# GpSimd's normalisation moved to step 6, and the PE's two score products of a step exchanged, in a two-layer transformer stack on one core

## The reference

```python
def _L0_attn_b_ref(x, Wqkv, Wo):
    qkv = (x @ Wqkv).reshape(b, l, 3, H, DH)          # H = 16 heads of DH = 16
    q, k, v = (qkv[:, :, 0], qkv[:, :, 1], qkv[:, :, 2])
    q = q * cos + rotate_half(q) * sin
    k = k * cos + rotate_half(k) * sin
    scores = jnp.einsum('bqhd,bkhd->bhqk', q, k) * scale
    attn = jax.nn.softmax(scores, axis=-1)
    out = jnp.einsum('bhqk,bkhd->bqhd', attn, v)
    return out.reshape(b, l, d) @ Wo
```

## Time and profile before

| what | value |
|---|---|
| runs | 2940.69, 2942.93, 2943.54 us (median 2942.93) |
| the profiled execution | 2938.81 us, of which the span is 2937.1 us |
| PE busy over the span | 2314.2 us (79%) |
| DVE, ACT, POOL busy | 1943.5 (66%), 1537.0 (52%), 912.0 us (31%) |
| granted PE clock, mean | 0.902 of full speed |
| stage rope | 967 to 1435 us |
| stage latent | 2152 to 2649 us |

### The profile page before, as it was taken

One profiled execution on the slowest core, in us unless ns is written; L12 is line 12 of the kernel. 1 busy time (PEld: TensorE's weight loads), 2 busy tenths in 40 slices (PEclk: granted clock), 3 DMA queues, 4 the chain that ended last, 5 costly groups with the idle time before them and its releaser, 6 DMA issues. The chain is left out here.

```text
span 2937.1 us, 40653 instructions
## 1 busy us (share of the span) xinstructions
PE 2314.2 (79%) x13550; PEld 1158.7 (39%) x13550; DVE 1943.5 (66%) x4549; ACT 1537.0 (52%) x2426; POOL 912.0 (31%) x851
## 2 busy tenths in 40 slices
PE   5899999998575899998756786399578788884698
PEld 2344444443452233332345555266322222223365
DVE  5788888886536888888463344577487677774343
ACT  2477766676523576777642333355146566672122
POOL 0333222230232344443033201355144445413111
PEclk7799999999887899999888898699779999996799
DMA  7665656550254112112126002454411211203232
GB/s 243 187 188 174 185 175 181 174 168 23 92 184 125 45 50 61 46 54 56 49 84 193 24 1 87 164 215 179 152 39 52 53 45 50 60 24 143 92 135 83
DMA packets 193506, 318.32 MB, mean 108 GB/s; under 512 B 29285, under 2 KB 155272, under 8 KB 188564
## 3 DMA queue, kind: packets, MB, share of 16 engines
q1 hardware_dynamic: 177764, 266.31, 29.1%
q0 software_dynamic: 15536, 49.41, 4.9%
HBM read 164.41 MB, written 151.59 MB: 108 GB/s over the span
## 5 line engine op out<-in xcount | busy, mean ns | idle before, releaser
L1816 DVE CUSTOM_DVE_ANT_0 decay_junk<-decay_scores_q,decay_corr 128x512 bf16<-128x512 f32 x512 | 338.3, 684 | 112.8 <-PE decay_scores_q L1553 110.6
L1733 ACT ACTIVATE decay_probs<-decay_scores_k 128x512 f32<-128x512 f32 x512 | 294.7, 597 | 190.4 <-PE decay_scores_k L1572 154.3
L2503 DVE TENSOR_REDUCE latent_mx<-latent_scores 128x2 f32<-128x1024 f32 x256 | 310.1, 1222 | 111.0 <-PE latent_scores L2292 110.7
L2426 ACT ACTIVATE latent_probs<-latent_scores,latent_escale 128x1024 f32<-128x1024 f32 x256 | 282.3, 1116 | 189.8 <-PE latent_scores L2305 189.0
L2426 ACT ACTIVATE rope_probs<-rope_scores,rope_escale 128x1024 f32<-128x1024 f32 x256 | 283.5, 1116 | 152.4 <-PE rope_scores L2305 151.6
L2503 DVE TENSOR_REDUCE rope_mx<-rope_scores 128x2 f32<-128x1024 f32 x256 | 311.1, 1223 | 78.7 <-PE rope_scores L2292 77.6
L1553 PE MATMUL decay_scores_q<-decay_KS,decay_QS 96*128 96x512 bf16 x512 | 204.8, 401 | 37.1 <-DVE decay_mx L1816 22.9
L1569 PE MATMUL decay_scores_k<-decay_QS,decay_KS 99*128 99x384 bf16 (+3 forms) x512 | 157.0, 308 | 14.4 <-DMA decay_QS<-decay_mT 6.6
L1597 PE MATMUL decay_out_heads<-decay_probs,decay_Vaug 128*32 128x512 f32 x1024 | 143.3, 633 | 0.8 <-DVE decay_probs L1828 0.8
L2318 PE MATMUL latent_out_heads<-latent_probs,latent_Vaug 128*32 128x512 f32 x1024 | 137.2, 608 | 6.7 <-ACT latent_Osb L2417 4.1
L2318 PE MATMUL rope_out_heads<-rope_probs,rope_Vaug 128*32 128x512 f32 x1024 | 137.2, 608 | 6.0 <-ACT rope_Osb L2417 4.1
(11 more groups left out here) (455 smaller groups left out, 5137.4 us busy)
## 6 DMA issues: line engine op xcount, KB each, us to landing
decay_KS<-decay_parts_dram SPq DMA_DIRECT2D x64, 384.0 KB
decay_QS<-decay_parts_dram SPq DMA_DIRECT2D x64, 384.0 KB
decay_parts_dram<-decay_parts SPq DMA_DIRECT2D x56, 384.0 KB, 3.1
experts3x_w<-in_w_dram SPq DMA_DIRECT2D x16, 1024.0 KB, 11.1
weight_parts<-experts3x_w SPq DMA_DIRECT2D x8, 2048.0 KB, 7.5
experts4x_w<-weight_parts SPq DMA_DIRECT2D x8, 2048.0 KB, 8.1
decay_parts_dram<-decay_parts SPq DMA_DIRECT2D x56, 256.0 KB, 3.3
experts_xin<-dispatched SPq DMA_DIRECT2D x96, 128.0 KB
```

The costliest lines, as they stand in the source:

```text
L1733: act.activation(probs[:, (b * 16 + kk) % PSLOTS, h, :], psB[:, s % 2, :], ACT.Exp, scale=scale).then_inc(exp_done, 1)
L1816: dve.tensor_tensor_reduce(junk[:, a % 2, :], psA[:, A_BANK[k], :], corr[:, qt, :], 1.0, -3.0e38, ALU.mult, ALU.max, mx[:, grp % 2, qt, h: ...
L2426: act.activation(probs[:, kk % 2, 2 * (u % 2):2 * (u % 2) + 2, :], psS[:, slot_of("exp", n), :, :], ACT.Exp, scale=escale[:, 0:1]).then_in ...
L2503: dve.tensor_reduce(mx[:, grp % 2, :, hp, qt], psS[:, slot_of("top", n), :, :], AX.X, ALU.max).then_inc(a_done, 1)
```

## The change

Two things. In both layers GpSimd normalises at step 6 and not at 18: behind its second rotary chain and not behind its third. And in each step the PE issues the score product for the maxima ahead of the one for the exponentials, with the list that gives out the PSUM slots changed alike. In `scores`, `top` is a tile for maxima and `exp` one for the exponential.

```diff
     ROTATE_AT = [2, 4, 16, 18]
-    NORMALISE_AT, PV_AT = 18, 1
+    NORMALISE_AT, PV_AT = 6, 1
...
     scores = [("top", n) for n in range(16)]
     for n in range(NB * STEPS):
-        scores += [("exp", n)] + ([("top", n + 16)] if n + 16 < NB * STEPS else [])
+        scores += ([("top", n + 16)] if n + 16 < NB * STEPS else []) + [("exp", n)]
     place = {x: i for i, x in enumerate(scores)}
...
             for b in range(NB):
                 for u in range(STEPS):
-                    exp_scores(b, u)
                     if top_of(b, u) is not None:
                         max_scores(top_of(b, u))
+                    exp_scores(b, u)
                     if u % 2 == PV_AT:
```

## The result

The changed kernel takes **2910.7 us** (median of six runs, 2906.7 to 2925.1); the kernel before took 2939.2 beside it (2935.6 to 2943.5). The ratio is 0.991, with the interval 0.9887 to 0.9932. Forecast were 2900 us within 2876 to 2924, faster. The profiled execution has a span of 2913.2 us, against 2937.1.

A forecast was written before the change was run, and what follows sets the result against it. The PE, fullest engine in rope and latent, was held by its standstills, chiefly a DMA wait in latent. -52 in latent, -5.8 in rope and +15 for the order gave -43 us: 2942.9 to 2900 us, range 2876 to 2924.

The forecast's parts named there:

- The long wait: Latent's batch boundaries: six PE waits for the row maxima's DMA, 37.4 us, caused by GpSimd normalising before its fourth chain.
- The clock term: Latent, PE work behind each long wait: the lower clock costs 2.66 us, six times, 16.0 us to be won back.
- The ports' rival: DVE's MV copies and row splits wait for GpSimd in crowded steps: +14 to +28 us, 2914 to 2928; chance 0.15.
- The order: Max scores ahead of exp scores in each step: costs 1.3 to 1.4 us a rope batch, 0.75 a latent batch, +15 us.
- the walk by start-to-start spacings: All 32 steps of a middle rope batch: new stalls not ACT's 4.7 us against 5.4; 1.56 lost behind the output additions.
- the sentence on latent: Latent has no q products: scalings cost nothing, steps 2 and 16 wait 0.4 more for a copy, +0.75 us a batch.
- below 1.2 us each: Both layers: the PE's other waits, for DVE or ACT to empty a PSUM bank or slot, are short, below 1.2 us.
- part 1: Normalise moved to step 6 in GpSimd's idle time: -52 us in latent (45 to 55) and -5.8 in rope.
- What would show it: Confirming signs: DMA wait gone, exp scores' waits for maxima 30 us or more per layer, latent near 450, rope within 6 of 468.
- signs that I was wrong: A DVE copy at L2545 over 0.17, third chain later than step 16's shuffle, or rope shorter by over 8 us.
- The order is cheap or a gain: Rival: the exchanged score order costs zero (2885 us) or wins 1 us a batch (2869); chance 0.20.
- Slower: Rival: exp scores make the PE pay all DVE work, +96 us, 2981; decides from 3.6 us a batch; chance 0.04.

The follow-up runs named there:

- norm_only: The changed kernel with normalise still at step 6 but the old order of the score products: 2882.5 us.
- norm_tripled: norm_only, with GpSimd in latent writing sixteen more normalised halves into an unread spare tile ahead of the real ones: 2919.9 us.
- order_only: The changed kernel with the new order of score products but normalise back at step 18: 2939.4 us, ratio 1.0005 to the kernel before.
- rotate_later: The changed kernel with the DVE's third and fourth rotation at steps 17 and 19 instead of 16 and 18: 2905.0 us.
- change_again: The changed kernel run once more without an edit, for its spread and a second profile: 2905.1 us.
- statistics_later: The changed kernel with the statistics of the two output additions put off to steps 15 and 17 of the next batch: 2898.1 us.
- heads_first: norm_only, with the DVE emptying the turned heads ahead of the step's maxima: 2860.1 us.
- sums_first: heads_first, with the addition to X also ahead of the maxima and its statistics behind them: 2843.6 us, ratio 0.9671 to the kernel before.

## Why the prediction was right, and where it wasn't

**The long wait: right.** The boundary's chain (GpSimd's normalisation ahead of the fourth chain, the parts' writes ahead of the rows' in SP's queue) was the cause; norm_only removes the wait whole and norm_tripled, by filling the same idle time, brings it back. Latent -47.2 lies within my 45 to 55, rope -7.2 beside the 5.8. The clock term holds in kind: the two steps behind a 6.6 us wait took 2.66 us more, the product behind 3.8 us 1.5 more. In size it was too large: of the 47.2, 37.4 are the waits themselves, which leaves 9.8 and not 16.0 for the clock and all else. I allowed only 1.4 for what is won back behind a wait; that the rest is such gain is inferred from the difference.

**The ports' rival: there, but too small to count.** The copies to MV (L2545), of the whole run and both layers: minimum, median and maximum in ns.

```profile
L2545 DVE COPY X<-rope_mv x16: 170/170/171, 1047.7 to 1454.7; 128x4 f32<-128x4 f32 x16
L2545 DVE COPY X<-latent_mv x16: 170/171/505, 2243.5 to 2638.6; 128x4 f32<-128x4 f32 x16
```

The medians hide some longer ones. Fifteen of the 32 copies began while a TENSOR_SCALAR of GpSimd ran. Nine of them kept their 0.17, and six, all in latent, took 0.28 to 0.51, five of these until 0.02 to 0.03 us behind the end of GpSimd's instruction. Here are the two of one batch; the normalisation, shown above, ends at 2359.05 + 6.51 = 2365.56:

```profile
2361.08 0.17 DVE L2545 COPY X<-latent_mv 128x4 f32<-128x4 f32 x1
2365.31 0.29 DVE L2545 COPY X<-latent_mv 128x4 f32<-128x4 f32 x1
```

So the neighbours that I priced at nothing cost 1.0 us of DVE time in all, within the upper bound that I had named and far from the rival's 14 to 28. Beside a TENSOR_TENSOR of GpSimd the effect is larger: the split of order_only took 2.22 us beside the 2.36 of the bias. The Trainium skill (SBUF — State Buffer, "Who interferes with whom") says that, when a DVE instruction in a two-port mode and one of GpSimd meet, whichever of the two issues first has the shared pair for its whole instruction while the other is fully blocked; the 2.22 beside 2.36 agrees and so do five of the longer copies, the 0.17 beside GpSimd's TENSOR_SCALAR does not.

**The order: right in sign, wrong in size.** In a middle batch of rope it costs 60.39 - 59.16 = 1.23, forecast 1.3 to 1.4; so the walk by start-to-start spacings was good to 0.1. In latent it costs 58.74 - 57.18 = 1.56, forecast 0.75. The step that failed is the sentence on latent, in which I carried rope's walk over, took the cost of the scalings off and added 0.4 at each idle step. From the first exp scores of a step to those of the next, in a middle batch, the change is longer than norm_only by (us):

```
           steps 0-15   16-19   20-31   batch
rope          0.47       0.39    0.38    1.24
latent        0.46       0.71    0.39    1.56
```

So latent saves nothing on the scalings that it doesn't have: up to step 15 and from step 20 on it pays what rope pays. The rest is at steps 16 to 19, where the split and the shuffle hold up the maxima and the exp scores of step 18 wait 0.60 us; rotate_later takes 0.50 of it back.

A second term wasn't in the sum of the order at all, the clock. The walk found the 1.56 us wait at step 13 and counted it once. Here it is as measured in rope's second batch (PE), and busy time with the granted clock (the last three numbers are clock, DMA share and GB/s) just behind it and in rope's end:

```profile
1053.31 0.39 PE L2305 MATMUL rope_scores<-rope_QS,rope_KS 50*128 50x512 f16 x2 [1.40 <-DVE rope_mx L2503]
1053.63 1.78 PE L2318 MATMUL rope_out_heads<-rope_probs,rope_Vaug 128*32 128x512 f32 x8
1055.34 0.61 PE L2292 MATMUL rope_scores<-rope_KS,rope_QS 48*128 48x512 f16 x2
1055.74 0.63 PE L2305 MATMUL rope_scores<-rope_QS,rope_KS 50*128 50x512 f16 x2
1056.31 2.44 PE L2265 MATMUL rope_work<-rope_xnT,rope_wk 128*128 128x512 f32 x4
```

```profile
1056.00:1060.00 4.00, 4.00 (x18) 1.15 (x16) 2.11 (x2) 1.79 (x2) 0.00 (x0) 0.84 0.00 0
1428.00:1440.00 12.00, 9.90 (x56) 2.07 (x52) 0.68 (x2) 8.62 (x11) 0.00 (x0) 0.72 0.00 0
```

Value sums take 1.78 instead of 1.06, scores 0.61 instead of 0.39: the engine is at the lower of its two levels (1.2 of 2.4 GHz) for some 3 us behind the wait, and the batch is 1.6 us longer. The same wait (1.29 to 1.40 us) stands in every batch but the first of both layers; the clock fell behind one in each layer. At the end of a layer value sums wait 2.1 us for ACT in norm_only too, there with a clock of 1.00 behind it, in rope of the change with 0.72 (second line). The kernel before has these waits as well, so the prediction's "below 1.2 us each" for the rest of the waits was not true of them. From the last batch's first value sums to its last it is 45.8 us instead of 41.8 in rope, 44.5 instead of 41.8 in latent. The old order has such a fall at times as well (43.4 in rope before), and change_again has 44.4 in rope, so not all of that is the order's.

The 28 us of the first profile, then: the six batches between first and last cost 9.1 in rope and 10.5 in latent, each with one fall of 1.6 in it; the last ones 3.9 and 2.6; the first ones 1.7 and 0.5. That is 28.3. Against my 15 the misses are latent's spacing (8.9 without the fall instead of 6 x 0.75, 4.4 more), the falls (3.2) and the last batches (6.5 instead of about 1.0); rope's spacing is 0.6 less than forecast (7.5 instead of 6 x 1.35), and the rest is rounding. Forecast for the whole were -43 us, measured are -28.5 by medians: about 3 us too much gain in part 1 and 13 too little cost in the order, which go the same way. That 2900 and 2910.7 lie nearer to each other than that is luck: the kernel before was taken at 2942.9 and measured at 2939.2.

**What would show it**: the DMA wait gone, right; rows' write right behind the transpose, right; waits of exp scores for maxima up to over 30 in each layer, 40.7 in latent, but 24.1 in rope, a miss; waits of max scores for exps gone, right; work banks waiting 0.2 to 0.3 for ACT, right in rope; latent's clock near 1.00, 0.98 from 2172 to 2627 us; latent near 450, measured 497 - 33.6 = 463, a miss by 13; rope within 6 us of 468, measured 468 + 7.6 = 475.6, a miss by 1.6. Both misses of time go one way, that of the order's price. Of the signs that I was wrong, one came: copies at L2545 longer than 0.17, six of them, 1.0 us of DVE time in all. The third chain wasn't late and rope wasn't shorter.

**The other rivals.** "The order is cheap or a gain" would have been the verdict from order_only, and is wrong where it counts. "Slower" needed 3.6 us a batch; 1.2 and 1.6 came in the change. With the heads emptied first the exchange costs 3.3 to 3.5, close to that in size; that its mechanism, all of the DVE's work paid by the PE, is then at work isn't shown.

## What to carry to other kernels

A long wait at an in-order queue is worth following back to the engine whose work sits in the wrong place. Here, moving that work into idle time removed the wait in full, and filling that time on purpose tested the claim. Time each part of a change alone and also on top of the other, since the second part looked free here only beside the fault that the first one repairs. Then look at what an in-order engine does ahead of the instruction that frees a buffer: emptying banks first took another 39 us off norm_only (2882.5 to 2843.6), which neither order of the PE's own score products did.

## What the runs showed of the hardware that I hadn't expected

- The granted clock of the PE can fall to the lower level behind a single wait of 1.4 to 1.6 us in an otherwise full stream (0.84 from 1056 to 1060 us), and costs 1.6 us then. It followed such a wait at two different steps (13 in the change, 17 in statistics_later's latent), and not in each batch that has one. No middle batch of norm_only, heads_first or sums_first had it. What decides in which batch it falls stays open.
- Behind the longer waits at the boundaries shown the product took 3.43 us (3.8 us of waiting) and 3.52 (2.8 us), against 1.98.
- A DVE TENSOR_SCALAR of 0.17 us was stretched to 2.22 beside one GpSimd TENSOR_TENSOR, and the SCALAR_TENSOR_TENSOR after it to 1.20 beside the next; beside GpSimd's TENSOR_SCALAR a copy kept its 0.17 in nine of fifteen cases and took 0.28 to 0.51 in six.
